# Half-megabyte weight transfers in a fused graph-network kernel on one core

## The chip, the cores and the metric

The kernel runs on 1 core of a Trainium2 chip. The metric is device time in microseconds (us) of one execution. Of the kernel before, three timed runs gave 245.12, 248.00 and 248.15 us: the median is 248.0 us. One further execution was profiled: it took 239.79 us, and its span from the first to the last instruction is 238.3 us.

## The reference, cut to what matters

The input is a graph of 96 nodes with 1024 features each. Two layers are computed, with a residual sum around each:

```
h = relu(layernorm(x))
q, k, v    = h @ wq.T + bq,   h @ wk.T + bk,   h @ wv.T + bv
q2, k2, v2 = q @ wiq.T + biq, k @ wik.T + bik, v @ wiv.T + biv    # then 16 heads of 64
attn = softmax(q2 k2^T / 8 + mask(edges, edge types))
x = x + (attn @ v2) @ wo.T + bo

h = relu(layernorm(x))
u = h @ root + bias + sum over 8 relations r of mean_r(h[src]) @ weight[r]
z = concat[u, h] @ w_gate + b_gate
x = x + tanh(u) * z + h * (1 - z)
```

All is float32. There are 18 weight matrices of 1024 x 1024 (the gate is two of them): 75.5 MB, each read once from HBM. The 96 node rows are few beside that, so each weight element takes part in 96 products.

## The kernel before, in words

**Layout.** Activations are kept transposed: features on the 128 partitions, 96 nodes along the free axis, eight feature chunks side by side (`hT`, `qT`, `kT`, `mean`, `uT`). A weight matrix is cut on the host into four *pieces* of 1 MB. A piece has 512 input features (four chunks of 128, the index `k`) by 512 output features (four chunks of 128, the index `c`). In HBM a piece is 128 rows of 8 KB, one for each partition: four runs of 512 floats, one for each `k`.

**The stream.** The queue of SyncE (SP) brings the 72 pieces in the order in which they are used (`SEQUENCE`, `KINDS`), each with one DMA (`fetch`, L237 to L241), into a ring of 12 slots in SBUF (`raw`). Each slot has one semaphore, `raw_landed[s]`, that rises by 16 when its piece has landed. The first 12 are issued at once; piece n waits until piece n-12 has been used (`piece_used`).

**TensorE.** The order of TensorE's work is written out by hand (L688 to L836). A call of `piece` (L588) waits for the landing and then runs 32 matmuls of the program: for each output chunk `c`, for each input chunk `k`, two halves `g` of 64 output features. A weight block of 128 x 64 is the stationary operand, 96 columns of the activations move. The trace shows each such matmul twice, so a piece is 64 weight loads and 64 matmuls there (4608 for the 72 pieces). The four pieces of a matrix accumulate in PSUM (`acc`), and VectorE takes each half of a result with its bias (`take`, L406).

**What lies between the pieces.** Transposes (L608, L615), the edge keys and codes (L628, L639), attention scores (L660), the turned probabilities (L667), the mixing of values (L683), the counting of edges by relation (L648) and the sums of messages (L787) stand between calls of `piece`. The eight relation matrices and the gate's second half (36 pieces, from 137.8 us on) follow one another with nothing between them.

**At the start.** The input x comes in two halves, one on SP's queue ahead of the weights and one on ScalarE's (ACT) queue; ACT's queue then brings biases, edge lists and type weights. Layer norm on VectorE and GpSimd, transposes on TensorE and a ReLU on ScalarE come before the first piece.

Of the kernel before, what the change touches and what calls it, by code (L numbers as in the profile page):

```python
# [14 lines left out]
P = 128  # L15
# [14 lines left out]
SLOTS = 12  # L30
# [8 lines left out]
def gnn_kernel(nc, x, weights, biases, edge_columns, edge_rows, type_weights, out):  # L39
    N, D = x.shape  # L40
    C = D // P
    HALF = D // 2
    CH = C // 2
    R = RELATIONS
    HEADS = 16
    HD = D // HEADS
# [13 lines left out]
    with ExitStack() as ctx:  # L60
        def sb(name, shape, dt=F32):
            return ctx.enter_context(nc.sbuf_tensor(name, shape, dt))

        def sem(name):
            return ctx.enter_context(nc.semaphore(name))

        raw = sb("raw", [P, SLOTS, CH * HALF])
# [65 lines left out]
        rows_landed = sem("rows_landed")  # L133
        edges_landed = sem("edges_landed")
        types_landed = sem("types_landed")
        raw_landed = [sem(f"raw_landed{s}") for s in range(SLOTS)]
        out_landed = sem("out_landed")
        piece_used = sem("piece_used")
        consts_ready = sem("consts_ready")
# [67 lines left out]
        def first_piece(m):  # L207
            return PIECES * SEQUENCE.index(m)
# [8 lines left out]
        def bank(t, b):  # L217
            return t[:, b, 0:TW]

        def half(t, b):  # L220
            return t[:, b * TW:(b + 1) * TW]

        def cols(t, b):
            return t[:, b * HALF:(b + 1) * HALF]
# [10 lines left out]
        @block.sync  # L235
        def _(sp):
            def fetch(n):  # L237
                where = PIECES * SEQUENCE[n // PIECES] + KINDS[n % PIECES]
                if n >= SLOTS:
                    sp.wait_ge(piece_used, n - SLOTS + 1)  # L240
                sp.dma_start(raw[:, n % SLOTS, :], weights[where]).then_inc(raw_landed[n % SLOTS], 16)  # L241

            sp.dma_start(cols(x_sb, 0), cols(x, 0)).then_inc(x_landed[0], 16)
            for n in range(N_PIECES):
                fetch(n)
            for b in range(2):
                sp.wait_ge(out_ready, b + 1)
                sp.dma_start(cols(out, b), cols(out_rows, b)).then_inc(out_landed, 16)
            sp.wait_ge(out_landed, 32)
# [337 lines left out]
        def _(pe):  # L587
            def piece(n, moving, a, opens=True, closes=True):  # L588

                s, kind = n % SLOTS, KINDS[n % PIECES]  # L590
                b, k0 = kind // 2, CH * (kind % 2)
                pe.wait_ge(raw_landed[s], 16 * (n // SLOTS + 1))
                for c in range(CH):
                    for k in range(CH):
                        for g in range(2):
                            at = k * HALF + c * P + g * HD
                            mm = pe.matmul(a[g * HD:(g + 1) * HD, b, c * N:(c + 1) * N], raw[:, s, at:at + HD],  # L597
                                           moving(k0 + k), start=opens and k0 == 0 and c == 0 and k == 0,
                                           stop=closes and k0 > 0 and c == CH - 1 and k == CH - 1)
                mm.then_inc(piece_used, 1)  # L600

            def of(t):
# [95 lines left out]
            n = first_piece(WQ)  # L698
            pe.wait_ge(h_ready, 1)
            piece(n, of(hT), acc[0])  # L700
            show_keys(0)
            piece(n + 1, of(hT), acc[0])
            show_keys(1)
            piece(n + 2, of(hT), acc[0])
            piece(n + 3, of(hT), acc[0])

            n = first_piece(WK)
# [6 lines left out]
            n = first_piece(WIQ)  # L714
# [9 lines left out]
            n = first_piece(WIK)  # L724
# [7 lines left out]
            n = first_piece(WV)  # L732
# [8 lines left out]
            n = first_piece(WIV)  # L741
# [17 lines left out]
            n = first_piece(WO)  # L759
# [31 lines left out]
            n = first_piece(ROOT)  # L791
# [6 lines left out]
            for b in range(2):  # L798
                mm = pe.matmul(bank(side, b), ones[0:N, :], half(counts, b), start=True, stop=True)
# [7 lines left out]
            n = first_piece(WG_X)  # L807
# [14 lines left out]
            for r in range(R):  # L822
                n = first_piece(REL0 + r)
# [5 lines left out]
            n = first_piece(WG_U)  # L829
# [45 lines left out]
```

## Time and profile before

| | |
|---|---|
| timed runs | 245.12, 248.00, 248.15 us; median 248.0 |
| profiled execution | 239.79 us, span 238.3 us |
| TensorE matmuls busy | 223.1 us, 94% of the span, 4823 matmuls |
| granted TensorE clock, mean | 0.997 of 2.4 GHz |
| VectorE, ScalarE, GpSimd busy | 64.9, 19.2 and 17.7 us |
| DMA | 77.0 MB, 323 GB/s over the span |
| first piece begins on TensorE | 9.2 us |
| last matmul of a piece ends | 233.1 us |

The profile gives each engine's busy time and what ended its idle time. "Issue" is time in which an engine waited for nothing that the profile shows. The DMA queue numbers stand for issuers: q1 is SP's queue (the weights), q10 is ACT's, and q8 carries packets of the kind "instruction".

### The profile page before, as it was taken

What the parts mean: (1) busy time and instruction counts of PE and PEld (TensorE: products, weight loads), DVE (VectorE), ACT (ScalarE), POOL (GpSimd) and SP (SyncE); (2) the same over time, 40 slices, a digit from 0 to 9 for tenths busy, and PEclk for the clock granted to TensorE, in tenths of its full rate; (3) what the DMA queues carried; (4) which work ended last, traced back from release to release, by engine and by line L of the source; (5) the groups of instructions that cost most, each with busy time, mean ns of one, the idle gap of its engine ahead of it and who ended that gap; (6) DMA issues with size and microseconds to landing.
All of it is one profiled execution on the core that took longest, in us unless ns stands there. A gap on an engine that the chain in (4) does not pass through costs nothing.

```text
span 238.3 us, 9967 instructions
## 1 busy us (share of the span) xinstructions
PE 223.1 (94%) x4823; PEld 213.0 (89%) x4823; DVE 64.9 (27%) x107; ACT 19.2 (8%) x31; POOL 17.7 (7%) x41
## 2 busy tenths in 40 slices
PE   2799998988999999989999999999999999999993
PEld 2689998888898989968899999999999999999992
DVE  2339512841386000061663340000000000000621
ACT  2531000000020031004100000000000000000101
POOL 2135000770000000010000000000000000000000
PEclk9999999999999999999999999999999999999998
DMA  6999999999999999982988779989999999600002
GB/s 215 390 396 422 422 419 421 421 418 418 417 419 418 418 417 408 362 360 76 314 320 267 267 234 392 399 330 380 400 417 418 411 403 411 245 3 3 3 3 69
DMA packets 11163, 77.00 MB, mean 323 GB/s; under 512 B 1450, under 2 KB 1522, under 8 KB 1908
## 3 DMA queue, kind: packets, MB, share of 16 engines
q1 hardware_dynamic: 10704, 76.09, 80.4%
q8 instruction: 38, 0.62, 1.0%
q10 hardware_dynamic: 420, 0.27, 0.4%
q14 instruction: 1, 0.01, 0.0%
HBM read 75.97 MB, written 0.39 MB: 320 GB/s over the span
## 4 chain that ended last, share of the span: by engine, by line
PE 92%; issue 2%; DVE 2%; DMA 2%; ACT 0%; POOL 0%; POOLq 0%
PE acc L597 82%; PE side L648 2%; DMA x_sb<-in_x 2%; PE turn L787 2%; PE side L787 1%; PE turn L615 1%; PE turn L608 1%; PE turn L683 1%; DVE stats L430 1%; PE side L660 0%; PE turn L660 0%; PE turn L667 0%; PE side L667 0%; DVE stats L546 0%; DVE rows L425 0%
## 5 line engine op out<-in xcount | busy, mean ns | idle before, releaser
L597 PEld LDWEIGHTS acc<-mean,raw 128*64 128x64 f32 x2048 | 84.5, 137 | 0.2 <-DVE mean L565 0.2
L597 PE MATMUL acc<-mean,raw 128*64 128x96 f32 x2048 | 84.7, 246 | 0.0
L597 PE MATMUL acc<-hT,raw 128*64 128x96 f32 x1536 | 68.9, 250 | 1.4 <-issue 0.8
L597 PEld LDWEIGHTS acc<-hT,raw 128*64 128x64 f32 x1536 | 65.6, 139 | 5.0 <-issue 3.4
L597 PE MATMUL acc<-qT,raw 128*64 128x96 f32 x512 | 23.1, 247 | 1.7 <-issue 1.7
L597 PEld LDWEIGHTS acc<-qT,raw 128*64 128x64 f32 x512 | 21.7, 137 | 2.6 <-issue 2.2
L410 DVE TENSOR_TENSOR uT<-acc,bias_cols 128x384 f32<-128x384 f32 x2 | 1.1, 558 | 81.9 <-PE acc L597 81.9
L597 PE MATMUL acc<-kT,raw 128*64 128x96 f32 x256 | 11.3, 247 | 1.6 <-issue 1.6
L597 PEld LDWEIGHTS acc<-kT,raw 128*64 128x64 f32 x256 | 10.8, 137 | 2.0 <-issue 2.0
L597 PE MATMUL acc<-uT,raw 128*64 128x96 f32 x256 | 10.7, 246 | 0.0
L597 PEld LDWEIGHTS acc<-uT,raw 128*64 128x64 f32 x256 | 10.6, 137 | 0.0
L390 ACT ACTIVATE gateT<-uT 128x384 f32<-128x384 f32 x2 | 1.0, 523 | 107.4 <-DVE uT L410 107.4
L410 DVE TENSOR_TENSOR kT<-acc,bias_cols 128x384 f32<-128x384 f32 x4 | 2.2, 558 | 15.5 <-PE acc L597 15.5
L565 DVE TENSOR_TENSOR mean<-turn,per_count 128x384 f32<-128x384 f32 x8 | 4.1, 553 | 7.8 <-PE turn L787 7.8
L648 PE MATMUL side<-mean,src_hot 102*96 102x384 f16 x32 | 5.9, 327 | 0.0
L483 DVE TENSOR_SCALAR mean<-node_iota,edge_tmp 102x768 f16<-102x768 f16 x16 | 5.9, 436 | 0.0
L608 PE MATMUL side<-ident,x_sb 96*128 96x96 f32 x8 | 1.5, 371 | 4.6 <-DMA x_sb<-in_x 4.6
L353 ACT ACTIVATE attn<-attn 96x768 f32<-96x768 f32 x2 | 1.7, 844 | 50.5 <-DVE attn L521 50.5
L608 PEld LDWEIGHTS side<-ident,x_sb 96*128 96x128 f32 x8 | 1.3, 224 | 4.6 <-issue 4.6
L559 DVE RECIPROCAL per_count<-per_count 128x192 f32<-128x192 f32 x4 | 5.0, 1309 | 0.0
L648 PEld LDWEIGHTS side<-mean,src_hot 102*96 102x96 f16 x32 | 3.7, 123 | 1.2
L565 DVE TENSOR_TENSOR mean<-side,per_count 128x384 f32<-128x384 f32 x8 | 4.1, 549 | 2.7 <-PE side L787 2.7
(128 smaller groups left out, 118.8 us busy)
## 6 DMA issues: line engine op xcount, KB each, us to landing
raw<-in_weights SPq DMA_DIRECT2D x72, 1024.0 KB, 8.2
out<-out_rows SPq DMA_DIRECT2D x2, 192.0 KB, 2.1
x_sb<-in_x ACTq DMA_DIRECT2D x1, 192.0 KB, 3.9
x_sb<-in_x SPq DMA_DIRECT2D x1, 192.0 KB, 3.7
bias_rows<-in_biases ACTq DMA_DIRECT2D x1, 36.0 KB
edge_i<-in_edge_columns ACTq DMA_DIRECT2D x1, 25.5 KB
mean<-in_edge_rows ACTq DMA_DIRECT2D x1, 12.8 KB
tw_in<-in_type_weights ACTq DMA_DIRECT2D x1, 1.5 KB, 13.1
```

Source lines behind the costliest of these rows:

```text
L353: act.activation(span, span, ACT.Exp).then_inc(exp_ready, 1)
L410: dve.tensor_tensor(by_chunk(half(dst, b)), by_chunk(bank(a, b)), bias_of(bias, b), ALU.add).then_inc(taken, 1)
L430: dve.bn_stats(stats[:, b, :], cols(x_sb, b)).then_inc(vec, 1)
L483: dve.tensor_scalar(rel_hot[:, c, :], node_iota[:, :], rel_key_f[:, c:c + 1], None, ALU.is_equal).then_inc(rel_hot_ready, 1)
L559: dve.reciprocal(span, span).then_inc(per_count_ready, 1)
L565: dve.tensor_tensor(mean[:, c, b * TW:(b + 1) * TW], bank((turn, side)[c % 2], b), half(per_count, b), ALU.mult).then_inc(mean_ready, 1)
L597: mm = pe.matmul(a[g * HD:(g + 1) * HD, b, c * N:(c + 1) * N], raw[:, s, at:at + HD], moving(k0 + k), start=opens and k0 == 0 and c == 0 a ...
L608: t = pe.transpose(dst[:, b, c * N:(c + 1) * N], src[:, (b * CH + c) * P:(b * CH + c + 1) * P], ident[0:N, 0:N])
L615: t = pe.transpose(dst[0:N, b, c * P:(c + 1) * P], src[:, (b * CH + c) * N:(b * CH + c + 1) * N], ident[:, :])
L648: mm = pe.matmul(side[0:N, b, 0:TW], src_hot[:, c, :], rel_hot[:, c, b * TW:(b + 1) * TW], start=c == 0, stop=c == EC - 1)
L683: mm = pe.matmul(turn[odd * HD:(odd + 1) * HD, h, j * N:(j + 1) * N], v2[0:N, head * HD:(head + 1) * HD], attnT[:, at:at + N], start=True, ...
L787: mm = pe.matmul(bank((turn, side)[c % 2], b), msgs[s][:, c * P:(c + 1) * P], half(counts, b), start=s == 0, stop=s == 1)
```

## The change

Each piece is brought by two DMAs in place of one. The first takes the first 4 KB of each of the 128 rows (input chunks k = 0 and 1), the second the other 4 KB (k = 2 and 3). Each slot gets two semaphores. `piece` waits for the first half, runs its 16 matmuls (all four `c` with k = 0, 1), waits for the second half and runs the other 16. The number of matmuls, their shapes and the slots are as they were; a slot is still free again only when the whole piece has been used.

```diff
-        raw_landed = [sem(f"raw_landed{s}") for s in range(SLOTS)]
+        raw_landed = [[sem(f"raw_landed{s}_{part}") for part in range(2)] for s in range(SLOTS)]
...
                 if n >= SLOTS:
                     sp.wait_ge(piece_used, n - SLOTS + 1)
-                sp.dma_start(raw[:, n % SLOTS, :], weights[where]).then_inc(raw_landed[n % SLOTS], 16)
+                for part in range(2):
+                    span = slice(part * CH * HALF // 2, (part + 1) * CH * HALF // 2)
+                    sp.dma_start(raw[:, n % SLOTS, span],
+                                 weights[where][:, span]).then_inc(raw_landed[n % SLOTS][part], 16)
...
-                pe.wait_ge(raw_landed[s], 16 * (n // SLOTS + 1))
-                for c in range(CH):
-                    for k in range(CH):
-                        for g in range(2):
-                            at = k * HALF + c * P + g * HD
-                            mm = pe.matmul(a[g * HD:(g + 1) * HD, b, c * N:(c + 1) * N], raw[:, s, at:at + HD],
-                                           moving(k0 + k), start=opens and k0 == 0 and c == 0 and k == 0,
-                                           stop=closes and k0 > 0 and c == CH - 1 and k == CH - 1)
+                for part in range(2):
+                    pe.wait_ge(raw_landed[s][part], 16 * (n // SLOTS + 1))
+                    for c in range(CH):
+                        for k in range(part * CH // 2, (part + 1) * CH // 2):
+                            for g in range(2):
+                                at = k * HALF + c * P + g * HD
+                                mm = pe.matmul(a[g * HD:(g + 1) * HD, b, c * N:(c + 1) * N], raw[:, s, at:at + HD],
+                                               moving(k0 + k), start=opens and k0 == 0 and c == 0 and k == 0,
+                                               stop=closes and k0 > 0 and c == CH - 1 and k == CH - 1)
                 mm.then_inc(piece_used, 1)
```

SP's whole program before: one DMA of x, twelve pieces without a wait, sixty that wait for a slot, and the output.

```order
L243 DMA x_sb<-in_x 96x512
L241 DMA raw<-in_weights 128x2048 x12
L241 DMA raw<-in_weights 128x2048 [waits piece_used] x60
L248 DMA out<-out_rows 96x512 [waits out_ready] x2
L60 UNCONDITIONAL_BRANCH [waits out_landed]
```

The same of the change, its first rows:

```order
L246 DMA x_sb<-in_x 96x512
L243 DMA raw<-in_weights 128x1024 x24
L243 DMA raw<-in_weights 128x1024 [waits piece_used]
L243 DMA raw<-in_weights 128x1024
L243 DMA raw<-in_weights 128x1024 [waits piece_used]
L243 DMA raw<-in_weights 128x1024
```

24 DMAs of half the size now go out without a wait, and after that each wait for a slot is followed by two of them.

TensorE at its first two pieces, before (`raw_landed0` and `raw_landed1` are the semaphores of slots 0 and 1):

```order
L597 MATMUL acc<-hT,raw 64x96 [waits raw_landed0,h_ready]
L597 MATMUL acc<-hT,raw 64x96 x31
L628 MATMUL turn<-out_rows,key_mul 102x408 [waits row_ready,edges_ready,h_ready]
L628 MATMUL turn<-out_rows,key_mul 102x408
L597 MATMUL acc<-hT,raw 64x96 [waits raw_landed1]
L597 MATMUL acc<-hT,raw 64x96 x31
```

The same place in the change:

```order
L601 MATMUL acc<-hT,raw 64x96 [waits raw_landed0_0,h_ready]
L601 MATMUL acc<-hT,raw 64x96 x15
L601 MATMUL acc<-hT,raw 64x96 [waits raw_landed0_1]
L601 MATMUL acc<-hT,raw 64x96 x15
L632 MATMUL turn<-out_rows,key_mul 102x408 [waits row_ready,edges_ready,h_ready]
L632 MATMUL turn<-out_rows,key_mul 102x408
L601 MATMUL acc<-hT,raw 64x96 [waits raw_landed1_0]
L601 MATMUL acc<-hT,raw 64x96 x15
```

A piece has become two runs of 16 matmuls with a wait at the head of each; nothing has moved between pieces.

## Rows read from the trace of the kernel before

**Rows 1.** The page: busy us (share of the span) xinstructions of each engine.

```profile
PE 223.1 (94%) x4823; PEld 213.0 (89%) x4823; DVE 64.9 (27%) x107; ACT 19.2 (8%) x31; POOL 17.7 (7%) x41
```

**Rows 2.** Windows of us, all work: length, busy (instructions) of each engine, clock, DMA share, GB/s.

```profile
0.00:9.20 9.20, 3.25 (x19) 2.71 (x19) 3.47 (x7) 2.00 (x3) 2.67 (x14) 1.00 0.76 271
9.20:30.00 20.80, 20.80 (x449) 19.95 (x450) 11.39 (x10) 5.94 (x9) 5.76 (x13) 1.00 1.00 413
30.00:76.00 46.00, 41.95 (x951) 39.97 (x949) 22.48 (x44) 1.69 (x2) 8.54 (x12) 1.00 1.01 418
...
143.00:202.00 59.00, 59.00 (x1436) 59.00 (x1434) 0.00 (x0) 0.00 (x0) 0.00 (x0) 1.00 0.99 396
202.00:238.00 36.00, 32.28 (x762) 31.65 (x758) 6.60 (x12) 2.23 (x4) 0.00 (x0) 0.99 0.16 60
```

**Rows 3.** The chain that ended last, in order of time: start, us, what.

```profile
0.81 3.69 DMA x_sb<-in_x
...
9.24 4.04 PE acc L597 x64
...
17.02 13.68 PE acc L597 x328
30.70 0.24 issue
30.94 5.44 PE acc L597 x127
36.38 0.69 issue
...
49.66 5.50 PE acc L597 x128
...
61.45 0.53 issue
61.98 0.71 PE acc L597 x11
62.69 0.85 PE side L660 x16
...
73.77 0.53 issue
...
137.88 95.22 PE acc L597 x2304
```

**Rows 4.** TensorE's waits, all of the span: us in total, times, longest.

```profile
PE acc L597 <- issue: 4.0, 7, 0.8
PE turn L608 <- DVE rows L425: 1.3, 1, 1.3
```

**Rows 5.** The page's DMA queues: packets, MB, share of 16 engines.

```profile
q8 instruction: 38, 0.62, 1.0%
```

**Rows 6.** DMA queues in the window 30 to 76 us.

```profile
q1 hardware_dynamic: 2626, 19.12, 100.2%
q8 instruction: 7, 0.11, 1.0%
```

**Rows 7.** The weight DMAs issued in 30 to 76 us: KB each, median us to landing.

```profile
raw<-in_weights SPq DMA_DIRECT2D x14, 1024.0 KB, 19.6
```

**Rows 8.** The same for those issued in 143 to 202 us.

```profile
raw<-in_weights SPq DMA_DIRECT2D x23, 1024.0 KB, 7.0
```

**Rows 9.** The page's other DMA issues: KB, us to landing.

```profile
out<-out_rows SPq DMA_DIRECT2D x2, 192.0 KB, 2.1
...
tw_in<-in_type_weights ACTq DMA_DIRECT2D x1, 1.5 KB, 13.1
```

**Rows 10.** DMA queues in 1.5 to 3.3 us; q10 moves mostly 2 KB rows of x.

```profile
q10 hardware_dynamic: 93, 0.15, 22.9%
```

**Rows 11.** Windows, L597 alone: length, PE busy, PEld busy, clock, DMA share, GB/s.

```profile
0.00:9.20 9.20, 0.02 (x2) 0.02 (x2) 1.00 0.76 271
9.20:30.00 20.80, 19.99 (x444) 19.62 (x446) 1.00 1.00 413
30.00:76.00 46.00, 39.60 (x903) 37.66 (x901) 1.00 1.01 418
```

**Rows 12.** Weight DMAs issued in 0 to 8.9 us: durations on the queue, first and last start; landing.

```profile
L241 SPq DMA_DIRECT2D raw<-in_weights x12: 417/432/2763, 1.2 to 8.8; - x12
...
DMA to landing us min/median/max: 6.3/19.0/28.1
```

**Rows 13.** Timelines of DVE and PE around the turned probabilities: start, us, instruction.

```profile
72.03 0.95 DVE L530 TENSOR_TENSOR attn<-attn,row_inv 96x768 f32<-96x768 f32 x1
...
76.27 0.86 PE L667 MATMUL side<-ident,attn 96*96 96x96 f32 x8
```

## The prediction

> **What bounds the kernel now.** I read the engines' busy times first: TensorE's matmuls are busy for 94% of the span, in 4823 records [rows 1]. The chain of waits then says whether that is work or queueing: from the first piece at 9.24 us it is TensorE almost without a break, and from 137.88 us on one unbroken run of 2304 matmuls in 95.22 us, 41.3 ns each, 2.65 us a piece of 64 [rows 3]. No step of the chain in that stretch is a landing of weights. TensorE's waits agree: the longest group, 4.0 us in 7 times, is "issue", which is no DMA of the program and no other engine [rows 4].
>
> The windows show the weights running ahead. By 30 us the DMA engines have moved 9.2 x 271 + 20.8 x 413, 11.1 MB [rows 2]; some 0.5 MB of that is x and the small tables, so about 10 pieces of 1.05 MB have come, and TensorE has used 446 matmuls, 7.0 pieces [rows 11]. By 76 us another 19.2 MB have come, 28 pieces, against (446 + 903) / 64 = 21 used. The DMA engines are full in these stages (418 GB/s, share 1.01) because 12 slots are being filled, not because TensorE lacks data.
>
> What then are the seven issue waits? Four views together answer it. Between them lie 127 or 128 matmuls of TensorE [rows 3]; the page has 38 packets of the kind "instruction" with 0.62 MB [rows 5], and 4823 / 38 = 127 matmuls, each with its weight load; in 30 to 76 us there are 7 such packets and 7 waits [rows 6, 4]. So I take them for waits for TensorE's own program, which the same DMA engines load. They come while the weight queue is deep (19.6 us from issue to landing) [rows 7] and not in 143 to 202 us, where the rate is nearly as high, 396 GB/s, but the queue shallow (7.0 us) [rows 8]. The waits end at 30.94, and after five more at 61.98 us: one load takes 31.04 / 5 = 6.2 us there, while its 127 matmuls are work for 127 x 41.3 ns = 5.25 us. The Trainium skill (Runtime: NRT & Kernel Launch, Instruction fetch mechanics) gives the same size, blocks of 256 instructions, but calls the cost of crossing one "mostly hidden". By that rule the 4.0 us would be something else and the change could not touch them; that is rival B.
>
> **The change part by part.** *TensorE's order.* 64 weight loads and 64 matmuls a piece as before, 128 x 64 by 96 columns; `c` and `k` change places outside of the pair `g`. 0 us. The 72 added waits stand on matmuls; the 72 old ones already stand so, 35 of them inside the unbroken run with its 41.3 ns [rows 3]. 0 us while the data is early.
>
> *SP's queue.* 72 more DMA instructions. SP needs 0.43 us for one while the first are issued [rows 12], 0.86 us for two halves, against 2.51 us that a piece takes to move (1.049 MB at 418 GB/s). Nothing else stands on that queue but x, which is ahead, and the output, which comes long after. 0 us. The first piece lands at 1.2 + 6.3 = 7.5 us, TensorE begins it at 9.24 [rows 12, 3], after layer norm. So the earlier first half buys nothing: 0.
>
> *Packets of 4 KB for 8 KB.* The trace has no 4 KB packet. Above stand the 8 KB ones: 19.12 MB in 1.002 x 16 x 46 = 737 us of engine time, 25.9 GB/s an engine [rows 6]. Below stand the 2 KB ones: 0.15 MB in 0.229 x 16 x 1.8 = 6.6 us, 22.7 GB/s [rows 10]. So a piece costs from 2.51 to 2.86 us; a cost of each packet plus one of each byte, drawn through both (0.316 us for 8 KB, 0.090 for 2 KB), gives 0.166 for 4 KB, or 2.63 us a piece, which I take. Does it bind? TensorE needs 2.65 us a piece where it is dense. By 30 us 10.1 pieces would become 9.6, or 8.9 at the worst end, for 7.0 used and one in use. 0 us; the cover is the lead of three pieces at 30 us, and it is gone only when the stream is 8 / 10.1 of today's, near 330 GB/s. The Trainium skill (DMA: Bandwidth & Descriptors, iDMA fabric) has 408.7 GB/s for a stream of 4 KiB rows; by that a piece would take 2.57 us, with the same result.
>
> *Turns on the DMA engines.* Everything on another queue shares engines with weight packets. How dear that is with a deep queue is shown by the 1.5 KB of `tw_in`, which took 13.1 us, where 192 KB of output on quiet engines took 2.1 us [rows 9]. With packets of 0.166 us for 0.316 us each turn waited for is about half. If the instruction load waits by turns, 0.95 us too much in a cycle of 6.2 us vanishes as soon as 0.95 / 0.15, six to seven turns, stand in that cycle, and 20 would fit. Bounds for this term: -4.0 us (all issue waits) and, if it waits for bytes, a loss: the bytes come 5% slower, 0.3 us on each of 7 cycles, +2 us. I take -3.5: the row nearest to the state after is 143 to 202 us, where the load keeps up and no wait is left, less a little for a rest.
>
> What is late next? The probabilities are ready at 72.03 + 0.95 = 72.98 us and TensorE turns them at 76.27 [rows 13]. Both hang on TensorE's scores at 62.69 us, and of the waits only 0.53 us lie between [rows 3], so some 2.7 us of cover stay. After 137.88 us there is only TensorE.
>
> Sum on the profiled execution: 0 + 0 + 0 - 3.5, 239.8 to 236.3 us. The timed median, 248.0 us, is 8.2 us above the profiled execution and shows no rows; I subtract the same 3.5 and get 244.5 us. A measurement here can tell about 2%, 5 us, from no change.
>
> **The rivals.** *B, the waits stay:* the load waits for bytes, or the issue waits are something else. For it: the time to landing differs between the stages in bytes too, and a packet of 16 KB (0.62 MB in 38) is itself longer than any turn. Against it: `tw_in`. Result 248, from 247 to 250.
>
> *C, the timed runs hold more of the same:* the 8.2 us between the profile and the median may be program loads that are late in the other stages too. Weights stream until 202 us, before which lie (4823 - 762) / 127 = 32 of the 38 loads [rows 1, 2]; 0.26 us more on each is 8.2 us. In the dense run the margin is thin, since the same load under a deep queue is 0.95 us too slow. With shorter turns most of it would go too: 248 - 3.5 - 5 = 239.5, from 236 to 242.9. For it is that the three runs differ by 3 us among themselves, as late loads would; against it, that no row shows it.
>
> *D, slower:* the stream falls under TensorE's need. Each half reads 4 KB of every 8 KB of HBM, and all 16 engines do so in step; if that or the doubled number of transfers costs more than the 2 KB rows suggest, the stream becomes the bound. It decides from the point where 3 + 72 r + 8 us passes the present 239.8. The 3 is the start of the stream (11.1 MB at 413 GB/s before 30 us), r the time of a piece, and 8 the last half piece (1.3), what follows 233.1 us in the span (5.2) and what lies around it (1.5). That is r = 3.18 us or 330 GB/s, 21% below today. At 320 GB/s it is 247 us in the profile, 255 in the median; at 300 GB/s 263 and 271. Against it: even the 2 KB rows lose only 12% for each byte, and q1's packets now fill 100.2% of 16 engines, with no gap between transfers that a second transfer would double. The Trainium skill (DMA: Bandwidth & Descriptors, Bandwidth) has a rule that speaks for D: batch to 1 MiB or more, since each DMA carries a fixed 2 us. Taken as exposed, it would give 2 x (2.0 + 1.2) = 6.4 us a piece and far over 400 us; the row of 100.2% shows it hidden by the queue.
>
> **How the numbers follow.** Forecast A (waits gone, nothing else) 0.40, at 244.5 with a range of its own from 242.8 to 246. B 0.26, C 0.24, D 0.10. The range of 8 in 10 takes A, B but for its upper edge and the upper part of C: 237.5 to 249.5; left out are D and C's lowest part. Faster by more than 2% (under 243.0) is C and the edge of A: 0.24 + 0.05 = 0.29. Within 2% is the rest of A and B: 0.61. Slower is D, 0.10.
>
> **What would show each step.** In the changed kernel's chain the issue waits between 30 and 76 us should be gone or total under 1 us, and the run of relations still take 95.2 us. The weight stream should hold 395 to 415 GB/s in 30 to 70 us; `tw_in` should land in 7 to 9 us in place of 13.1. No wait of TensorE for `in_weights` should appear. Wrong would be: issue waits of 4 us as before (B), a rate under 340 GB/s with waits for weights (D), or a profile near 236 with a median near 240 (C).

## The result, and the profile after

The change is slower: 20 timed runs give a median of 251.1 us (247.8 to 254.5), 20 of the kernel before 242.8 us (238.9 to 248.6). The medians stand as 1.034 to 1. Each ratio given with an interval compares, of both kernels, only the runs within 1.5% of the kernel's fastest: here 1.039, with a 95% interval from 1.034 to 1.043. The 248.0 us that the prediction started from was the upper part of a wide spread. The profiled execution of the change took 251.83 us, near its median, against 239.79 of the kernel before, 3 us under its median. So the 12 us between the two profiles are more than the 8.3 us between the medians, and the sizes are checked below on other executions with the same transfers.

TensorE's waits in the trace of the change (us in total, times, longest) answer to [rows 4]:

```profile
PE acc L601 <- issue: 13.8, 16, 1.8
PE side L612 <- DMA x_sb<-in_x: 4.3, 1, 4.3
PE turn L612 <- DVE rows L428: 1.4, 1, 1.4
```

The issue waits grew from 4.0 to 13.8 us, and there is still no wait for weights. The chain of the change (start, us, what) shows where; it answers to [rows 3]:

```profile
30.83 0.48 issue
31.32 5.44 PE acc L601 x127
36.76 0.68 issue
...
138.54 16.23 PE acc L601 x389
154.77 0.99 issue
155.76 5.50 PE acc L601 x128
161.26 0.42 issue
...
180.12 1.79 issue
181.91 5.50 PE acc L601 x128
...
207.65 0.42 issue
208.07 37.03 PE acc L601 x891
```

Before 143 us the waits are what they were, 4.5 us in 7 for 4.0 in 7. What was one run of 95.22 us without a break is now cut nine times between 154 and 208 us, every 128 matmuls, for 9.3 us in all. The run and its breaks together take 106.6 us. The rest of the difference, 106.6 - 95.2 - 9.3 = 2.1 us, lies in the restarts after the waits: 128 matmuls between two waits take 5.50 us, where the unbroken run needs 128 x 41.3 ns = 5.29. So 9.8 us of waits and 2 us of restarts are the 12.0 us between the two profiles.

That the issue waits are waits for TensorE's own program can be seen packet by packet. The instruction queue of the change in 153 to 154.3 us, just ahead of the first late wait (154.77 to 155.76):

```profile
q8 instruction: 1, 0.02, 4.6%
```

One packet of 16 KB ends there, at 154.27 us, and TensorE goes on at 155.76. At all nine late waits such a packet ends 1.2 to 1.5 us before TensorE goes on, and it takes 0.9 to 1.0 us itself, as elsewhere. Its own time is the usual one; it starts late.

The weight stream in 30 to 76 us, DMA queues first (packets, MB, share of 16 engines), then the issues (KB, us to landing), for [rows 6, 7]:

```profile
q1 hardware_dynamic: 5106, 18.60, 101.6%
q8 instruction: 7, 0.11, 1.0%
...
raw<-in_weights SPq DMA_DIRECT2D x35, 512.0 KB, 15.8
```

The same two rows for 143 to 202 us, for [rows 8]:

```profile
q1 hardware_dynamic: 5346, 19.49, 94.6%
...
raw<-in_weights SPq DMA_DIRECT2D x38, 512.0 KB, 6.4
```

The number of issues in a window times their time to landing, over the window's length, is about the mean number of transfers in flight. Before it was 14 x 19.6 / 46 = 6.0 in the first window and 23 x 7.0 / 59 = 2.7 in the second [rows 7, 8]. In the change it is 12.0, and then 38 x 6.4 / 59 = 4.1. Counted transfer by transfer in the traces it is 7.5 and 2.6 before, and 12.2 and 4.1 in the change. In bytes the second window holds no more than before (2.1 MB for 2.8). In transfers it holds half as many again.

### The profile page after: what moved, and what is told of

It reads as the page before. It is cut to its first block, busy times and chain, and to the rows that moved or that the text cites. A ratio compares the mean times of both kernels' runs of the same rounds, so it can differ in the third digit from the quotient of the medians.

```text
span 250.1 us, 10039 instructions
## 1 busy us (share of the span) xinstructions
PE 225.5 (90%) x4823; PEld 214.0 (86%) x4823; DVE 64.8 (26%) x107; ACT 19.1 (8%) x31; POOL 17.7 (7%) x41
## 4 chain that ended last, share of the span: by engine, by line
PE 89%; issue 6%; DVE 2%; DMA 1%; ACT 0%; POOL 0%; POOLq 0%
PE acc L601 79%; PE side L652 2%; PE turn L791 1%; DMA x_sb<-in_x 1%; PE side L791 1%; PE turn L619 1%; PE turn L612 1%; PE turn L687 1%; DVE stats L433 1%; PE side L664 0%; PE turn L664 0%; PE turn L671 0%; PE side L671 0%; DVE stats L549 0%; DVE rows L428 0%
## 5 line engine op out<-in xcount | busy, mean ns | idle before, releaser
L601 PE MATMUL acc<-mean,raw 128*64 128x96 f32 x2048 | 86.7, 246 | 9.3 <-issue 9.3
```

## The experiments

All ratios are to the kernel before, run on the same chip beside it. Two theories stood at first. **S**: packets of 4 KB make TensorE's program loads late. **N**: twice the number of transfers does. A third, **O**, is TensorE's new order.

**e1, the order alone.** One DMA and one wait a piece; in `piece` the loop over `part` stays.

```diff
-                for c in range(CH):
-                    for k in range(CH):
+                for part in range(2):
+                    for c in range(CH):
+                        for k in range(part * CH // 2, (part + 1) * CH // 2):
```

> One DMA and one semaphore a piece as before; only TensorE's order is that of the change (all c with k = 0, 1, then k = 2, 3). If the size of the packets or the number of transfers makes TensorE's program loads late (theories S and N), this is the kernel before: ratio 0.99 to 1.01, issue waits 4 us and none after 143 us. If the order of the matmuls does it (theory O), ratio near 1.04 with some 9 us of issue waits after 150 us.

Measured: 1.001 [0.995, 1.008]. The order costs nothing. Its trace says one thing more about the kernel before, whose work this is: 6.1 us of issue waits, of which two (0.75 and 0.97 us) stand at 201.75 and 208.00 us. So late waits can come in an execution without any change. They may be part of the spread of 10 us; no trace of one of the long executions of the kernel before shows it.

**e2 and e10, packets of 4 KB alone.** The host lays a piece out as two blocks of 128 rows of 4 KB.

```diff
-                sp.dma_start(raw[:, n % SLOTS, :], weights[where]).then_inc(raw_landed[n % SLOTS], 16)
+                sp.dma_start(raw[:, n % SLOTS, :].rearrange("p (h c) -> p h c", h=2),
+                             weights[where].rearrange("h p c -> p h c")).then_inc(raw_landed[n % SLOTS], 16)
```

> One DMA of 1 MB a piece, but in packets of 4 KB: the host lays each piece out as two halves of 128 rows of 4 KB, and the DMA gathers them. TensorE as before. Theory S (packet size makes the loads late): ratio near 1.04, about 9 us of issue waits after 150 us. Theory N (number of transfers): ratio 0.99 to 1.01 and a weight stream of 407 GB/s in 30 to 76 us without consequence.

> One DMA a piece in packets of 4 KB, again, with more rounds: its first ratio, 1.0135, had an interval from 0.99 to 1.03. If packet size and number of transfers add up (theory S+N), 1.01 to 1.02. If the number alone matters, 0.995 to 1.005; if the size alone, as the change.

Measured: 1.0135 [0.992, 1.035], and with more rounds 1.009 [1.004, 1.014]. That is about a third of what the change costs on the same chip (e9, below), but the medians of all runs differ by 0.2% only. The trace of e10 (244.45 us) has 407 GB/s in 30 to 76 us, and 2.7 us of issue waits after 143 us. The trace of e2 (247.63 us, its longest execution) has twice as much there:

```profile
PE acc L598 <- issue: 5.4, 6, 1.5
```

Both had 2.5 transfers in flight in 143 to 202 us, no more than the kernel before. So smaller packets make late waits without any more transfers.

**e3, two transfers of 8 KB packets, by halves of the partitions.**

```diff
+                for part in range(2):
+                    half_p = slice(part * P // 2, (part + 1) * P // 2)
+                    sp.dma_start(raw[half_p, n % SLOTS, :],
+                                 weights[where][half_p, :]).then_inc(raw_landed[n % SLOTS][part], 16)
```

> Two DMAs of half a megabyte a piece, but in packets of 8 KB: each takes 64 of the 128 partitions; TensorE waits for both and keeps its order. Theory N (twice the transfers make the loads late): ratio near 1.04. Theory S (packet size): ratio 0.99 to 1.01, stream 418 GB/s.

Measured: 332.7 us. The run tells nothing on N, because another thing broke: the stream ran at little more than half its rate, and TensorE's issue waits came to 50.8 us in 24 times beside 17.4 us of waits for weights. DMA queues of e3 in 30 to 76 us:

```profile
q1 hardware_dynamic: 1626, 10.67, 100.6%
```

10.67 MB in 1.006 x 16 x 46 = 740 us of engine time is 14.4 GB/s an engine, where 8 KB packets to all 128 partitions had 25.9 [rows 6].

**e5 and e11, the same by even and odd partitions.**

```diff
-                    sp.dma_start(raw[half_p, n % SLOTS, :],
-                                 weights[where][half_p, :]).then_inc(raw_landed[n % SLOTS][part], 16)
+                    sp.dma_start(raw[part:P:2, n % SLOTS, :],
+                                 weights[where][part:P:2, :]).then_inc(raw_landed[n % SLOTS][part], 16)
```

> Two DMAs of half a megabyte a piece in packets of 8 KB, now each with every second partition (0, 2, 4, ... and 1, 3, 5, ...), so that all 16 engines write all over the partitions; TensorE waits for both and keeps its order. Theory N (twice the transfers make the program loads late): ratio 1.02 to 1.04 with a stream near 418 GB/s. Theory L (the loads are late where the weight stream leaves the DMA engines no idle time; 4 KB packets matter since they take 3% of the capacity): ratio 0.99 to 1.01. If the stream again falls under 300 GB/s, the split by partitions is itself dear and the run tells nothing on N.

> Two DMAs a piece in packets of 8 KB on every second partition, again on the same chip as the change. Theory S+N: 1.01 to 1.02. Size alone: 0.995 to 1.005. Number alone: as the change.

Measured: 1.0136 [1.007, 1.020] and 1.012 [1.006, 1.018], at 419 GB/s. So the number of transfers costs about 1.2% at full stream rate; the medians of all runs differ by 2.0% in e5 and 0.1% in e11. The traces have 2.3 and 1.0 us of issue waits after 143 us, where the kernel before has none. Both intervals lie above 1, which speaks against theory L in the expectation (the loads miss idle time on the engines, and only the packets' 3% matters); e6, below, speaks against it more plainly.

**e4, e12 and e9, the change's transfers with TensorE's old order, and the change again.** e4 and e12 wait for both halves ahead of a piece.

> The transfers of the change exactly, but TensorE waits for both halves ahead of a piece and keeps the order of before. Theories S and N both: ratio 1.03 to 1.045 as the change itself, since no half is ever awaited. Theory O: ratio 1.00.

> The changed kernel itself, as the yardstick on this chip for the next three. By the earlier result a ratio of 1.035 to 1.045, with issue waits of 8 us or more after 143 us.

> The change's transfers with TensorE's old order and both waits ahead of the piece. If the transfers are all of the loss, the same ratio as the change within 0.5%. If the waits inside a piece or the order add to it, 1% or more below the change (the first runs, on different chips, had 1.025 against 1.039).

Measured: e4 1.025 [1.012, 1.039], e12 1.025 [1.020, 1.030], e9 1.029 [1.020, 1.038]. On that one chip size (0.9%) and number (1.2%) add up to 2.1%, both together cost 2.5%, and the change itself 2.9%. With intervals of 0.5 to 0.9 to either side these can't be told apart; the medians of all runs give 0.2, 0.1, 1.5 and 2.3%, by which the two together cost more than their sum. The transfers are the loss; how it divides is not settled by the times. TensorE's waits in the trace of e12 (247.47 us), all of the span and then from 143 us on:

```profile
PE acc L601 <- issue: 9.6, 14, 1.3
```

```profile
PE acc L601 <- issue: 3.8, 6, 1.3
```

So 5.6 us more waits than before, and with a restart of 0.2 us for each of 7 more, 7.0 of the 7.7 us between this profile and [rows 4]'s.

**e13, no stream in the dense run.** The change, with `for part in range(2 if n < 48 else 0)` in `fetch`: the last 24 pieces are not brought, and TensorE's waits for them ask only for the last landing that their slot has had. It leaves out a third of the weights, so its output is not the kernel's.

> The change, but the last 24 pieces are not brought: TensorE works through the pieces that stand in the slots, with all its waits and in the same order (the last 24 of 72 pieces are the wrong weights). If the weight stream makes the program loads late, the issue waits after 150 us go from 8 or 9 us to 0 and the waits before 143 us stay at 4.4 us: ratio about 0.995. If the added waits or the order in TensorE's program do it, they stay and the ratio is 1.03.

Measured: 1.0005 [0.996, 1.005]; issue waits 4.6 us, all before 143 us. TensorE ran all of the change's waits and the same instructions. Windows of e13, for [rows 2]:

```profile
143.00:202.00 59.00, 59.00 (x1436) 59.00 (x1434) 0.00 (x0) 0.00 (x0) 0.00 (x0) 1.00 0.01 3
```

The late waits come from the weight stream beside TensorE's loads and from nothing in TensorE's program.

**e6, e7, e16 and e17: the kernel before with at most three, two or four pieces in flight.** Shown for two:

```diff
+                if n >= 2:
+                    sp.wait_ge(raw_landed[(n - 2) % SLOTS], 16 * ((n - 2) // SLOTS + 1))
```

> The kernel before, but SP issues piece n only when piece n-3 has landed: at most three transfers of 1 MB in flight. Theory Q (a deep weight queue makes the program loads late): the 4 us of issue waits in 30 to 76 us go, ratio 0.98. Theory L (busy engines, not depth): three in flight still fill the engines, the waits stay, ratio 1.00.

> The same with at most two transfers of 1 MB in flight. A transfer alone took 4.7 us from issue to landing in the trace of before, so the stream should fall to some 350 to 410 GB/s with short idle times on the engines. Theories Q and L both: issue waits fall below 2 us in all, ratio 0.97 to 0.985. If the waits stay at 4 us or more, neither depth nor load is the cause. If weights come too late, waits for them show and the ratio is over 1.

> The kernel before with at most two whole pieces in flight, again with more rounds. Ratio 0.975 to 0.985 as the first time, issue waits under 1 us; against a before whose runs hold late waits of their own it may reach 0.965.

> The kernel before with at most four whole pieces in flight. If the number of transfers in flight decides (theory F), four are as bad as four halves: 3 to 4.5 us of issue waits before 143 us; after it the slots alone keep the flight below three, so 0 to 2 us: ratio 0.99 to 1.01. If only the full queue of 7 or more did it, or if it is something special to halves, waits before 143 us are under 1 us as with three in flight, ratio 0.97 to 0.985.

Measured: four in flight 0.998 [0.993, 1.003]; two 0.980 [0.974, 0.986] and 0.973 [0.964, 0.982]; for three there is no ratio: its four runs took 235.3, 239.2, 241.0 and 246.3 us beside a median of 239.6, and the traced one is the 235.3. TensorE's issue waits in all of the span, with four, with three and with two:

```profile
PE acc L599 <- issue: 4.7, 8, 0.8
```

```profile
PE acc L599 <- issue: 0.5, 1, 0.5
```

```profile
PE acc L599 <- issue: 0.2, 1, 0.2
```

Windows of 30 to 76 us (length, PE, PEld, DVE, ACT, POOL busy, clock, DMA share, GB/s), four and then three in flight:

```profile
30.00:76.00 46.00, 41.48 (x940) 39.50 (x938) 22.34 (x44) 1.69 (x2) 8.55 (x12) 1.00 1.01 419
```

```profile
30.00:76.00 46.00, 45.49 (x1058) 44.38 (x1054) 22.35 (x44) 2.50 (x3) 8.54 (x12) 1.00 1.01 412
```

The DMA engines are as full in both, share 1.01, and nearly as fast. With four transfers in flight the waits are those of the kernel before with its six to eight; with three they are gone and TensorE runs 118 matmuls more in the window. In these 46 us the number of transfers makes the difference, and not the load or the rate at which they are issued (18 in the window in both). That two are enough rests on timed runs too; that three are rests on this one trace, since the other three executions of e6 took 239.2 us and more.

**e8, e14 and e15: a limit with half transfers, and with 4 KB packets.** In e8 and e14 SP issues a half when the third, or the fourth, half before it has landed; e15 is e2 with two whole pieces in flight.

```diff
+                    m, other = divmod(2 * n + part - 4, 2)
+                    if m >= 0:
+                        sp.wait_ge(raw_landed[m % SLOTS][other], 16 * (m // SLOTS + 1))
```

> The changed kernel, but SP issues a half only when the third half before it has landed: at most 1.5 MB in flight. Theories Q and L: the 14 us of issue waits of the change fall to under 4, ratio 0.97 to 0.99. Theory N: the number of transfers is that of the change, so waits after 143 us stay and the ratio is 1.02 or more.

> The change with at most four halves, 2 MB, in flight. Landing of a half took 5.4 us with three in flight, so about 375 GB/s can come, enough that no weight is awaited. Theory F (what counts is how many bytes or transfers are in flight beside the load, as with two whole pieces): issue waits under 1.5 us in all, ratio 0.98 to 0.99. If four transfers are as bad as the four that were in flight after 143 us in the change, waits of several us stay there and the ratio is over 1.00.

> One DMA a piece in 4 KB packets with at most two in flight. Theory F: the waits go as with 8 KB packets, ratio 0.98 to 0.99; the stream some 350 GB/s in 30 to 76 us. If 4 KB packets delay the loads by themselves, waits of 2 us or more after 143 us stay and the ratio is 0.99 to 1.00.

Measured: e8 1.157 [1.150, 1.163], e14 1.004 [0.998, 1.011], e15 0.978 [0.971, 0.984]. In e8 I had misjudged the stream: 1.5 MB in flight gave 289 GB/s, no issue wait at all, and

```profile
PE acc L604 <- DMA raw<-in_weights: 31.0, 34, 2.7
```

e14 and e15 are a pair for the number alone. Both move 4 KB packets with 2 MB in flight; e14 as four transfers, e15 as two. Windows of e14 and then of e15:

```profile
30.00:76.00 46.00, 41.98 (x959) 40.52 (x956) 22.17 (x44) 1.69 (x2) 8.72 (x12) 1.00 0.95 340
143.00:202.00 59.00, 55.70 (x1318) 54.63 (x1316) 0.00 (x0) 0.00 (x0) 0.00 (x0) 1.00 0.96 348
```

```profile
30.00:76.00 46.00, 45.95 (x1074) 44.92 (x1072) 22.36 (x44) 2.50 (x3) 8.55 (x12) 1.00 0.95 348
143.00:202.00 59.00, 58.70 (x1417) 58.42 (x1414) 0.00 (x0) 0.00 (x0) 0.00 (x0) 1.00 0.95 350
```

Bytes in flight, packets, rate and share of the engines are nearly equal; TensorE is idle 4.0 and 3.3 us in e14's two windows, 0.05 and 0.3 us in e15's. The traced execution of e14 took 244.94 us, its median, and the ratios say the same: 2.7% lies between them. So with 4 KB packets four transfers in flight are worse than two of the same bytes. Two more things differ: e14 has TensorE's new order, which e1 priced at nothing, and its halves read 4 KB of every 8 KB of HBM, where the host of e15 has laid the 4 KB rows side by side. No run tests that second difference by itself.

**When the program's packet starts.** After a wait TensorE runs 256 instructions (254 in e5, e11, e12 and e4, whose second wait ahead of a piece makes TensorE's program longer). Counted on from the places of the waits, this gives the moment at which it enters each block of its program, in traces without waits too. The table has the median time from there to the start of the packet that brings the next block, in us, beside the transfers in flight counted one by one, and the issue waits after 143 us. Not in the table are e1 (3.8 us in the first window and 2.0 in the second), e16 (2.0 and 2.9), e8 (1.8 and 1.9) and e3 (6.0 and 5.7).

| runs | in flight, 30 to 76 | packet starts after | in flight, 143 to 202 | packet starts after | late waits |
|---|---|---|---|---|---|
| before | 7.5 | 3.7 | 2.6 | 2.1 | 0 |
| 4 KB packets alone: e10, e2 | 7.1 | 3.7 | 2.5 | 2.8, 3.1 | 2.7, 5.4 |
| two transfers alone: e11, e5 | 14 | 3.7, 3.8 | 4.0, 4.2 | 2.8, 2.7 | 1.0, 2.3 |
| both: e12, e4, e9, the change | 12 | 3.7 to 3.8 | 4.1 to 4.4 | 3.4, 3.2, 3.3, 4.1 | 3.8, 4.4, 7.9, 9.3 |
| no stream in the dense run: e13 | 12 | 3.7 | 0 | at once | 0 |
| four whole pieces: e17 | 4.0 | 3.8 | 2.2 | 1.6 | 0 |
| three: e6 | 3.0 | 2.5 | 2.3 | 1.8 | 0 |
| two: e7 | 2.0 | 2.1 | 2.0 | 1.5 | 0.2 |
| four halves: e14 | 4.0 | 3.4 | 4.0 | 3.1 | 3.9 |
| two pieces of 4 KB packets: e15 | 2.0 | 2.1 | 2.0 | 2.0 | 0.9 |

The delay grows gradually, and a wait is what goes over a margin. A block of 5.3 us without a wait, less 1.0 us for the packet and 1.2 to 1.5 us from its end until TensorE goes on, leaves about 3 us. Between 143 and 202 us, over all traces, none of the 107 packets that started less than 2.6 us after the block's beginning was waited for, and 40 of the 41 that started over 3.5 us after it were. In 30 to 76 us the delay rises from 2.1 to 2.5 to 3.8 us with two, three and four transfers of 1 MB in flight and is 3.7 or 3.8 with seven, 12 and 14 too, with packets of 8 or of 4 KB. In the dense run the kernel before stood at 2.1 us, 2.9 at the most. There packets of 4 KB alone added 0.7 to 1.0 us with no more transfers in flight, twice the transfers alone added 0.6 to 0.7, and both 1.1 to 2.0.

## Why the prediction was wrong

**TensorE's order, 0; SP's queue, 0; the earlier first half, 0: right.** e1 has 1.001. No weight was awaited in the change.

**Packets of 4 KB: the rate right.** I priced one at 0.166 us and the stream at 399 GB/s; measured were 407 GB/s, and the lead over TensorE held. That they cost nothing otherwise was wrong: e2 and e10 have late program loads by them alone. The Trainium skill's 408.7 GB/s for 4 KiB rows (DMA: Bandwidth & Descriptors, iDMA fabric) is nearer than my line through two rows.

**Turns on the DMA engines, -3.5 us: this is the step that failed.** It measured +9.8 us in issue waits, and about +2 us of restarts that had no term. (The 0.95 us too much in a cycle, from which the step counted its turns, held these restarts too: the five waits are 3.3 us, 0.65 each.) What the step took from `tw_in` came true of `tw_in`:

```profile
DMA to landing us min/median/max: 8.7/8.7/8.7
```

That is the landing of `tw_in` in the change, 8.7 us for 13.1 [rows 9], inside the 7 to 9 that I gave. Packets of 4 KB alone brought it to 10.4 and 10.3 us (e2, e10) and two transfers of 8 KB packets to 10.2 and 11.2 (e5, e11), so the turns are only a part of that too. TensorE's program load, one packet of 16 KB, did not follow: in 30 to 76 us it started 3.7 us after its block began with packets of 8 KB and with packets of 4 KB, and the waits before 143 us went from 4.0 to 4.5 us. In the dense run it started later with smaller packets, not earlier: 4.1 us for 2.1. I carried a price from one kind of transfer to another, and bounded the loss by +2 us with the bytes of the stream, which e14 and e15 show equal where the waits differ.

**The cause of the waits: right, and its reading half right.** That they are program loads stands: they go on every 127 or 128 matmuls, and vanish with the stream (e13). I had also seen that they come with a deep queue and not with a shallow one [rows 7, 8]. But I read depth as bytes and time, and took the absence of waits in the dense run for a state that would last. There the program's packet already started 2.1 us after its block began, with about 3 us of room. Half-size packets and twice the transfers, each worth some 0.6 to 1.0 us by itself, put it over that in a stretch of 59 us where TensorE has nothing else to wait for. The rule of the Trainium skill that spoke against the change, to batch to 1 MiB (DMA: Bandwidth & Descriptors, Bandwidth), had the sign right, though not by the fixed 2 us for each transfer (same page, Anatomy of one DMA) that the prediction gave as its reason: these did stay hidden, at a share of 101.6%. Its other rule (Runtime: NRT & Kernel Launch, Instruction fetch mechanics), that crossing a block of the program is mostly hidden, fits the traces in 30 to 76 us with three transfers or fewer in flight; with four or more it cost 4 us or more here in that window alone.

**The rivals.** D had the side right and the mechanism wrong; it is real, as e8 shows. Its sum 3 + 72 r + 8 with 289 GB/s, r = 3.63 us, gives 272 us, and e8's profile took 277. B was right for the part before 143 us. C was half right: late waits lay in one more execution of that kernel's work (e1), but the change added to them. No rival had the waits spread to the dense run, though I had called its margin thin under C.

**What stays open.** Why the program's packet starts later with more transfers in flight, up to four, and in the dense run with smaller packets, no view of the DMA queues shows. In the dense run the number in flight and the rate at which transfers are issued rose together, and no run parts them there. e16, with two in flight, has 3.0 us of late waits in one execution (below), so few transfers in flight are no guarantee. Two traces of the change had 9.3 and 7.9 us of late waits, where e12 and e4 had 3.8 and 4.4 with the same transfers; the timed ratios, 1.029 and 1.025, don't tell them apart, and I leave it there. The sizes rest on one trace of each run.

## A version that beats both

e7 and e16, two whole pieces in flight, are 2.0% and 2.7% faster than the kernel before; e15, with 4 KB packets, 2.2%. All three intervals lie under 1, though not wholly under 0.98. On the chip of e7 the medians are 235.7 us against 239.6; on that of e15 and e16 they are 237.2 and 238.2 against 242.9. The limit has a price on its other side. One execution of e16 (246.3 us) had only 316 GB/s in 30 to 76 us, and TensorE waited 5.4 us for weights, and 3.0 us for its program after 143 us:

```profile
PE acc L599 <- DMA raw<-in_weights: 5.4, 7, 1.3
...
PE acc L599 <- issue: 3.0, 3, 1.5
```

## What to carry to other kernels

Where a long program runs beside a deep stream of loads, look for waits at even distances in instructions: they may be the program's own loading, and here they depended on how many transfers were in flight and on the size of their packets, not on the bytes. A stretch that shows no such wait may still be close to one: measure the time to the start of the program's packet, not the wait that is left of it. Keep the in-flight count as low as the rate allows (here two or three of 1 MB), by letting the queue wait for an earlier landing; a smaller transfer is not a milder one. And price an effect on one kind of transfer only from a row of that kind.

## What the runs showed that I had not expected

The same 8 KB rows go at 419 GB/s in two transfers of even and odd partitions (e5) and at 232 GB/s (10.67 MB in 46 us) in two transfers of partitions 0 to 63 and 64 to 127 (e3). The Trainium skill (DMA: Bandwidth & Descriptors, The descriptor swizzle) says that the two halves of the partitions lie on different sets of 8 of the 16 ports; by its ceiling of 435 GB/s for all ports (same page, Specifications), eight would give 217 as an estimate, near what e3 shows and a little under it. The trace itself has no view of ports.
